# A twelve-stage decoder on one Trainium2 core: the quantised feed-forward stage with its weights quantised in the stage before, the gate's products first, and the gate's chain laid into up's products

## What is computed

```python
def act_qdq(x):
    scale = jnp.maximum(jnp.max(jnp.abs(x)) / 32767.0, 1e-12)
    return jnp.clip(jnp.round(x / scale), -32768.0, 32767.0) * scale
def fixed_qdq_u16(x):
    return jnp.clip(jnp.round(x * 65536.0), 0.0, 65535.0) / 65536.0
x = act_qdq(_layernorm(x))
up = act_qdq(x @ lpbq_dequant(w_up).T)       # weights in blocks of 32, 4 bits
gate = act_qdq(x @ lpbq_dequant(w_gate).T)   # 768 features each
sig = fixed_qdq_u16(jax.nn.sigmoid(gate))
gate = act_qdq(gate * sig)
o = act_qdq(gate * up)
return o @ lpbq_dequant(w_down).T            # added to x
```

## Time and profile before

| | |
|---|---|
| median of 3 runs | 2941.95 us (2939.73 to 2943.08) |
| profiled execution, its own time | 2943.42 us |
| its span | 2941.7 us |
| busy | PE 74%, DVE 60%, ACT 41%, POOL 19% |
| mean granted TensorE clock | 0.861 |

### The profile page before, as it was taken

The page is one execution under the profiler, slowest core; times in us unless marked ns, Lnnn a source line. Parts: engine busy times, 40 slices in busy tenths (PEclk is TensorE's granted clock), DMA queues, the critical chain, the costliest instruction groups (busy, mean ns, idle before and its releaser), DMA issues. The chain is left out here.

```text
span 2941.7 us, 28763 instructions
## 1 busy us (share of the span) xinstructions
PE 2190.0 (74%) x10262; PEld 1365.5 (46%) x10293; DVE 1775.1 (60%) x2543; ACT 1191.5 (41%) x1871; POOL 570.0 (19%) x332
## 2 busy tenths in 40 slices
PE   3788899694799889695648888887599483173794
PEld 2456556582233247574214444444357331162474
DVE  3455354425677555313669898987345656836765
ACT  1334322111466634111248898998132125301240
POOL 2231112121322110120105454642012000000100
PEclk8899799697899989697878999998699787586896
DMA  6644100253844000343000000001100000000001
GB/s 168 102 73 51 55 1 0 100 173 102 115 65 65 1 19 1 115 159 88 29 29 1 0 1 1 1 1 58 55 1 1 33 0 0 0 7 0 19 1 34
DMA packets 107530, 126.74 MB, mean 43 GB/s; under 512 B 14823, under 2 KB 98676, under 8 KB 106357
## 3 DMA queue, kind: packets, MB, share of 16 engines
q1 hardware_dynamic: 87444, 102.55, 15.8%
q10 hardware_dynamic: 17058, 14.79, 1.6%
q0 software_dynamic: 2880, 7.48, 0.7%
...
## 5 line engine op out<-in xcount | busy, mean ns | idle before, releaser
L2914 DVE TENSOR_TENSOR_SCAN l2s_h<-l2s_aw 128x2048 f32<-128x2048 f32 x64 | 283.5, 4430 | 3.3 <-PE l2s_c_ps L2863 2.7
L2871 PE MATMUL l2s_big<-g_xn,g_ident 128*128 128x512 f32 x512 | 266.8, 625 | 11.7 <-ACT g_xn L2947 5.8
L2928 POOL TENSOR_SCALAR l2s_aw<-l2s_aw 128x2048 f32<-128x2048 f32 x64 | 240.0, 3750 | 152.0 <-DVE l2s_aw L2906 147.1
L568 DVE TENSOR_REDUCE l1at_nm<-l1at_s 128x1 f32<-128x512 f32 x256 | 162.0, 684 | 63.9 <-PE l1at_s L418 62.9
L2863 PE MATMUL l2s_c_ps<-g_ident,l2s_h 128*128 128x128 f32 x1024 | 155.4, 287 | 45.7 <-ACT g_xn L2947 26.3
L2863 PEld LDWEIGHTS l2s_c_ps<-g_ident,l2s_h 128*128 128x128 f32 x1024 | 122.7, 147 | 141.3 <-issue 99.1
L2947 ACT ACTIVATE g_xn<-l2s_c_ps,l2sfr_ct 128x512 f32<-128x512 f32 x256 | 169.2, 736 | 35.0 <-PE l2s_c_ps L2863 33.9
L666 ACT ACTIVATE g_xn<-l1at_s 128x512 f32<-128x512 f32 x256 | 143.2, 598 | 81.8 <-PE l1at_s L442 81.3
L2906 DVE TENSOR_TENSOR l2s_aw<-l2s_dtu,l2s_b_ps 128x2048 f32<-128x2048 f32 x64 | 146.2, 2288 | 27.9 <-remote 22.1
L2940 ACT ACTIVATE l2s_aw<-l2s_dt,l2s_A 128x2048 f32<-128x2048 f32 x64 | 131.2, 2052 | 0.0
L568 DVE TENSOR_REDUCE l0at_nm<-l0at_s 128x2 f32<-128x384 f32 x128 | 70.1, 557 | 98.6 <-PE l0at_s L418 97.3
...
## 6 DMA issues: line engine op xcount, KB each, us to landing
...
```

Of the source, the lines that this page charges most:

```text
L568: V.tensor_reduce(nm[:, s % 2, qts[0]:qts[-1] + 1, r], s1[:, u % 3, 0:len(qts) * KEYS].rearrange("p (q k) -> p q k", k=KEYS), AX, ALU.max, ...
L2871: nc.tensor.matmul(acc[:, tb, :], ident[:], hCT[:, tb, :], start=n == 0, stop=n == NST - 1).then_inc(acc_done, 1)
L2914: V.tensor_tensor_scan(out=h_all[:, i % 2].rearrange("p c t -> p (c t)"), data0=dA[:, i % 2].rearrange("p c t -> p (c t)"), data1=wd[:, i ...
L2928: nc.gpsimd.tensor_scalar(wd[:, i % 3], wd[:, i % 3], 10.0, -10.0, ALU.min, ALU.max).then_inc(clipped, 1)
```

## The change

The weights get a scope of their own around both stages (`QuantisedBlocks`, tiles l2q). They are loaded by SP at the start of the cross-attention's tile loop, and VectorE quantises them in place in 15 pieces, one behind each tile's addition. `quantised_ffn` becomes one block, layer norm included. x's peak is taken over `xn`, two tiles at a time, between the tiles' scalings. Gate's products come before up's. Gate's chain (shift, back, sigmoid, round, clip, swish, peak) runs on VectorE, ScalarE and GpSimd while TensorE makes up's products; GpSimd does all of gate's backs, one shift, the clip (now one step, `cut`), and up's back. Up keeps no scale of its own: only the constant is subtracted, and the scales are folded into o's (`fold`). The subtraction of swish's constant goes into the product (`multiply`), the max with 0 and the product of sigmoid and gate into one operation (`swish`). The down product goes tile by tile: o is shifted and brought back 128 tokens at a time. `emptied` counts ScalarE's copies out of the ring of four banks.

```diff
+            if blocks is not None:
+                @block.sync
+                def _(sp):
+                    blocks.load(sp)
...
+                    if blocks is not None:
+                        blocks.quantise(dve, t)
...
+        if 0 < t <= 14:
+            dve.wait_ge(self.step, t)
+        if t < 3:
+            dve.wait_ge(self.loaded[t], 16)
+            v.tensor_reduce(self.peak[:, t], blocks(t), AX, ALU.max, apply_absolute_value=True).then_inc(self.step, 1)
+        elif t == 3:
+            v.tensor_scalar(self.peak[:], self.peak[:], 1.0 / 7.0, 1e-12, ALU.mult, ALU.max).then_inc(self.step, 1)
+        elif t == 4:
+            v.reciprocal(self.inv[:], self.peak[:]).then_inc(self.step, 1)
+        elif t < 8:
+            v.tensor_tensor(blocks(t - 5), blocks(t - 5), per_block(self.inv, t - 5), ALU.mult).then_inc(self.step, 1)
+        elif t < 10:
+            part = flat[:, (t - 8) * half:(t - 7) * half]
+            v.tensor_scalar(part, part, ROUND, ROUND, ALU.add, ALU.subtract).then_inc(self.step, 1)
+        elif t < 12:
+            part = flat[:, (t - 10) * half:(t - 9) * half]
+            v.tensor_scalar(part, part, -8.0, 7.0, ALU.max, ALU.min).then_inc(self.step, 1)
+        elif t < 15:
+            v.tensor_tensor(blocks(t - 12), blocks(t - 12), per_block(self.peak, t - 12), ALU.mult).then_inc(self.step, 1)
...
-            prepare(nc, name + "l", c, [
...
-                    ch.step(v.tensor_reduce(peak[:], blocks, AX, ALU.max, apply_absolute_value=True))
-                    ch.step(v.tensor_scalar(peak[:], peak[:], 1.0 / 7.0, 1e-12, ALU.mult, ALU.max))
-                    ch.step(v.reciprocal(inv[:], peak[:]))
-                    ch.step(v.tensor_tensor(qb, blocks, inv[:, :, None].to_broadcast([P, NB, QB]), ALU.mult))
-                    ch.step(v.tensor_scalar(q[:], q[:], ROUND, ROUND, ALU.add, ALU.subtract))
-                    ch.step(v.tensor_scalar(q[:], q[:], -8.0, 7.0, ALU.max, ALU.min))
-                    ch.step(v.tensor_tensor(qb, qb, peak[:, :, None].to_broadcast([P, NB, QB]), ALU.mult))
...
+        uses = [("w", n, j) for n in (1, 0) for j in range(FC // 2)] + [("xn", j) for j in range(PAIRS)]
+        uses += [("ff", 1, j) for j in range(NT)] + [("ff", 0, j) for j in range(NT)] + [("down", j) for j in range(FC // 2)]
+        number = {use: u for u, use in enumerate(uses)}
+        shifter = "dddaap"
...
+                def take(*use):
+                    u = number[use]
+                    if u >= 4:
+                        pe.wait_ge(emptied, u - 3)
+                    return ring[:, u % 4, :]
...
+                for n in (1, 0):
+                    for j in range(FC // 2):
+                        turn_w(n, j)
+                for g in range(PAIRS):
+                    turn_xn(g)
+                turn_peak(X)
+                spread(X)
+                for j in range(NT):
+                    if j < NBLK:
+                        pe.wait_ge(x_quantised, j + 1)
+                    product(1, j)
+                product(0, 0)
+                turn_peak(GATE)
+                product(0, 1)
+                spread(GATE)
+                for j in range(2, NT):
+                    product(0, j)
+                for j in range(FC // 2):
+                    turn_down(j)
+                for n in (UP, SWISH, OUT):
+                    turn_peak(n)
+                    spread(n)
+                pe.wait_ge(emptied, number["down", FC // 2 - 1] + 1)
                 for t in range(TILES):
-                    if t % QT == 0:
-                        pe.wait_ge(o_ready, t // QT + 1)
+                    pe.wait_ge(o_ready, t + 1)
...
+                def scaled_tiles(g):
+                    for i in (2 * g, 2 * g + 1):
+                        v.tensor_scalar(xn[:, i, :], x[:, i, :], mean[:, i:i + 1], rstd[:, i:i + 1], ALU.subtract, ALU.mult).then_inc(xn_ready, 1)
+                def peak_of(n, col, a):
+                    return v.tensor_reduce(peaks[:, n, col:col + 1], a, AX, ALU.max, apply_absolute_value=True)
+                def peak_of_tiles(g):
+                    dve.wait_ge(xn_ready, 2 * g + 2)
+                    return peak_of(X, g, flat_xn[:, 2 * g * DM:(2 * g + 2) * DM])
+                scaled_tiles(0)
+                for g in range(1, PAIRS):
+                    scaled_tiles(g)
+                    peak_of_tiles(g - 1)
+                ch.step(peak_of_tiles(PAIRS - 1))
...
+                shift_x(0)
+                for b in range(NBLK):
+                    if b + 1 < NBLK:
+                        shift_x(b + 1)
+                    back_x(b)
...
+                for m in range(FC):
+                    if shifter[m] == "d":
+                        v.tensor_scalar(gate[:, m, :], gate[:, m, :], scale[:, GATE, 1:2], ROUND, ALU.mult, ALU.add).then_inc(shifted["d"], 1)
...
+                def swish(m):
+                    dve.wait_ge(sig_cut, m + 1)
+                    v.scalar_tensor_tensor(out=gate[:, m, :], in0=sig[m % 3], scalar=0.0, in1=gate[:, m, :], op0=ALU.max, op1=ALU.mult).then_inc(swish_made, 1)
+                def swish_peak(m):
+                    dve.wait_ge(swish_made, m + 1)
+                    return peak_of(SWISH, m, gate[:, m, :])
+                for m in range(FC - 1):
+                    peaks_of_products(UP, up, 0, m)
+                    swish(m)
+                    swish_peak(m)
+                ch.step(peaks_of_products(UP, up, 0, FC - 1))
+                begin_scale(UP, NT)
+                swish(FC - 1)
+                row_of_scale(UP, 1e-12)
+                end_scale(UP)
+                ch.step(swish_peak(FC - 1))
+                begin_scale(SWISH, FC)
+                row_of_scale(SWISH, 65536e-12)
+                end_scale(SWISH)
+                v.tensor_scalar(gate[:, 0, :], gate[:, 0, :], scale[:, SWISH, 1:2], ROUND, ALU.mult, ALU.add).then_inc(swish_shifted_d, 1)
+                ch.step(v.tensor_scalar(fold[:, 0:1], row[0:1, SWISH, 0:1], row[0:1, UP, 0:1], 1.0 / 65536.0, ALU.mult, ALU.mult))
+                ch.step(v.tensor_scalar(fold[:, 1:2], fold[:, 0:1], 1.0 / QMAX, None, ALU.mult))
...
+                def multiply(m):
+                    if m == 0:
+                        dve.wait_ge(swish_shifted_d, 1)
+                    else:
+                        dve.wait_ge(swish_shifted, m)
+                    dve.wait_ge(up_back, m + 1)
+                    v.scalar_tensor_tensor(out=up[:, m, :], in0=gate[:, m, :], scalar=ROUND, in1=up[:, m, :], op0=ALU.subtract, op1=ALU.mult).then_inc(product_made, 1)
...
+                shift_o(0)
+                for t in range(TILES):
+                    if t + 1 < TILES:
+                        shift_o(t + 1)
+                    back_o(t)
+                    if t >= 2:
+                        add(t - 2)
...
+            @block.gpsimd
+            def _(pool):
+                def back(m):
+                    wait_shifted(pool, m)
+                    nc.gpsimd.tensor_scalar(gate[:, m, :], gate[:, m, :], ROUND, scale[:, GATE, 0:1], ALU.subtract, ALU.mult).then_inc(gate_back, 1)
+                def cut(m):
+                    pool.wait_ge(sig_rounded, m + 1)
+                    nc.gpsimd.tensor_scalar(sig[m % 3], sig[m % 3], ROUND + 65535.0, ROUND, ALU.min, ALU.subtract).then_inc(sig_cut, 1)
+                back(0)
+                back(1)
+                nc.gpsimd.tensor_scalar(gate[:, FC - 1, :], gate[:, FC - 1, :], scale[:, GATE, 1:2], ROUND, ALU.mult, ALU.add).then_inc(shifted["p"], 1)
+                for m in range(FC):
+                    if m + 2 < FC:
+                        back(m + 2)
+                    cut(m)
+                for m in range(FC):
+                    pool.wait_ge(up_shifted, m + 1)
+                    nc.gpsimd.tensor_scalar(up[:, m, :], up[:, m, :], ROUND, None, ALU.subtract).then_inc(up_back, 1)
...
+                done = 0
+                for j in range(NT):
+                    empty(up[:, j // NBLK, j % NBLK * BANK:(j % NBLK + 1) * BANK], "ff", 0, j)
+                    if j == 2:
+                        shift_gate(3)
+                    elif j == 3:
+                        shift_gate(4)
+                    while done < 2 * FC and 4 + done * 20 // (2 * FC) <= j:
+                        if done % 2 == 0:
+                            sigmoid(done // 2)
+                        else:
+                            round_sigmoid(done // 2)
+                        done += 1
...
+                shift_up(0)
+                shift_up(1)
+                for m in range(1, FC):
+                    shift_swish(m)
+                    if m + 1 < FC:
+                        shift_up(m + 1)
...
+        with Scope(nc, "l2q") as S8:
+            blocks = QuantisedBlocks(nc, S8, of("L2_ffn_")) if stage(8) else None
+            if stage(7):
+                l2x = of("L2_xattn_")
+                c["norm"] = ("l2b", (l2x["g_x"], l2x["b_x"]))
```

(3 more changed lines are left out.)

327 lines of the change are left out of this document (181 added, 146 removed).

## The result

| | before | after |
|---|---|---|
| median | 2942.51 us (4 runs, 2939.73 to 2943.92) | 2895.85 us (4 runs, 2891.41 to 2898.39) |
| ratio to before | | 0.9844, 95% interval 0.9831 to 0.9858 |
| profiled execution, its own time and span | 2943.42, 2941.7 us | 2897.5, 2895.8 us |
| mean granted TensorE clock | 0.861 | 0.869 |

What follows compares the result with a forecast made beforehand. Stage 8 was read as stretches bound alternately by VectorE and TensorE, so overlap was the gain: last addition from 2610.68 to 2521.9, 88.8 us less 0.5, gives 2855.1 profiled, 2854 us median (3.0% faster), range 2846 to 2872.

Steps and rivals of the forecast that it cites:

- Weights in the loop, cost nothing: Cross-attention loop: weight-quantising pieces hide in 3.7 us of slack, turn stays 7.76 us; only the last tile costs 0.5.
- Up to the first product: From cross-attention's last addition to gate's first product: terms sum to 23.8 us, first product at 2330.0, 34.8 us earlier.
- Gate's products, T: Gate's products take 43.0 us, to 2373.0; gate's scale follows 4.4 us later, at T = 2377.4.
- Down: Down product after o's scale: 1.95 us of pieces, 16 tiles in 41.4, slow start 2.5; last addition at 2521.9.
- the rival of the low clock: TensorE granted no more than 0.50 in both product phases and down: slower than before, 2972 if all is lost; 1%.
- one sign of being wrong: Listed signs against the forecast included TensorE waiting for ScalarE's copies of up and a granted clock under 0.9 in products.
- GpSimd's price: GpSimd operations on 128x2048 floats: 1.9 us of work each, from the scan's clip, excluding VectorE's two-input and double-rate operations.
- gate's scale to swish's: Gate's chain beside up's products, VectorE the bound after its first swish: 62.7 us, swish's scale at 2440.1.
- swish's scale to o's: VectorE's shift, fold, six products and peaks, and o's scale: 35.3 us where before took 40.15, ending at 2475.4.
- GpSimd slow by itself: GpSimd's operations take 3.8 us of their own: first cut ends at T+20.3, time 2858 to 2866; 8%.
- The change doesn't overlap: Up's products stall on ScalarE, whose chain waits for GpSimd; up's 41 us come on top, 2895; 2%.
- The lock falls badly every time: Each of six swishes and six multiplies waits a whole 1.9 us GpSimd operation, 22.8 us in all: 2872; 12%.

Runs made afterwards that it cites:

- short pairs: The changed kernel with all three kinds of GpSimd pieces rewritten as operation pairs measured short (add/multiply, min/max), cut's offset moved into VectorE's multiply: 2836.86 us, 0.9651 of before.

## Why the prediction was wrong

**What held.**
- *Weights in the loop, cost nothing*: turn 7.76 us, 23.2 us more when they are taken out.
- *Up to the first product*: forecast 2330.0, measured 2328.06. Of the 1.9 us, 0.9 is an earlier start of the scalings (2313.76 for 2314.68), with a hand-over between the stages of 0.35 us, and 1.0 that two scalings and a peak took 1.24 us where the sum has 1.36, eight times.
- *Gate's products, T*: forecast 2377.4, measured 2376.30 (2376.14 and its 0.16).
- *Down*: from o's scale to the last addition forecast 46.5 us, measured 46.4. The terms that the prediction writes out (1.95, 41.4, 2.5) make 45.9; the other 0.6 has no term of its own there, and the last addition takes 0.42.
- *Clock*: 0.95 in gate's products, 0.93 in down; the rival of the low clock didn't come. In up's products one sign of being wrong did show: behind TensorE's waits for a bank (3.7 to 6.0 us) the granted clock fell from 0.98 (2389.00 to 2405.70) to 0.70 (2434.17 to 2451.00), between its two levels of 2.4 and 1.2 GHz. With short pairs, where it works on, it was 1.00 up to 2415. Swish's scale did not wait for it.

**What failed** is the step "GpSimd's price": "So I take 1.9 us for work". It took the scan's clip as the price of any scalar operation on 128x2048 floats. The clip is min/max, one of the four short pairs found; only one of the change's 19 GpSimd operations (the shift) has a short pair. Of the twelve backs and cuts the first took 9.2 us, beginning beside VectorE's shifts, and the others 7.1 to 7.2; the six of up took 5.7 in the mean. Two terms carry the miss:

| stretch | forecast | change | short pairs |
|---|---|---|---|
| gate's scale to swish's | 62.7 | 103.3 | 58.2 |
| swish's scale to o's | 35.3 | 41.7 | 34.0 |

That is 40.6 and 6.4 us, 47.0. T was 1.1 us early, so the last addition came 45.8 us after its forecast of 2521.9 (2567.68). The profiled execution came only 42.4 us after its own forecast (2897.5 for 2855.1): 0.5 is the allowance for the last tile, and 2.9 lie behind the stage, where the same code took 328.1 us for 331.0. With short pairs both terms come out a little under the forecast, and TensorE makes up's products there in 38.0 us without a gap, so the rest of the two sums held as a whole: the order of work, ScalarE's and TensorE's room, VectorE as the bound behind the first swish.

The price reached the time in two ways. Up to the last cut it is GpSimd's own pace. From swish's scale to o's it is the lock: VectorE works 40.1 of the 41.7 us and no multiply waits for its piece of up, but the shift takes 4.17 us and five of the six multiplies 5.31 or 3.40 in place of 2.28, beside the long pieces of up.

The rival "GpSimd slow by itself" named the right mechanism, and had too small a price: it took 3.8 us, the median of the clip in the scan, as GpSimd's own time. Its sum for the first cut, "five operations and 1.3", gives T + 34.0 with what the five took (9.2, 7.2, 2.0, 7.2, 7.1, and 1.4). The row showed how long one form takes; nothing in the profile of before bounded the others from above. The rival "The change doesn't overlap" is half of what happened: TensorE did stall on ScalarE's copies behind GpSimd. But up's products were through at 2440.4, 39 us ahead of swish's scale, so they did lie beside the chain. That the measured time is beside this rival's 2895 is chance: its 41 us were to be up's products, and the 47 are GpSimd's.

**The lock** was the part that the prediction weighed against a page. In the change a swish is held by a back: it starts 0.03 us after the back's start and ends 6.71 us after it. The Trainium skill, page "SBUF — State Buffer", section "Who interferes with whom", has the loser block for the whole instruction and keeps reductions out of it. The runs agree on reductions, and on copies and scalar operations (6.9 of 7.1 us); they differ for two-input operations, which were let through at 4.4 of 7.1. By its rule a swish would by estimate have taken 7.1 + 2.3 less 0.03, 9.4 us, where 6.68 was measured.

How much a lock costs depends on the length of what holds it, so the short pairs removed most of it too: in the fastest version the longest swish is 3.43 us and the longest multiply 3.54. The rival "The lock falls badly every time" had the count nearly right for the change and the price wrong: four of six swishes (6.59 to 6.68 us) and five of six multiplies are held, for 1.1 to 4.4 us each and not for 1.9. The holds of the first three swishes are hidden, since VectorE waits 2.85 us for the next cut all the same; behind the fourth it waits for no cut any more, so that hold is part of the 40.6 us.

**What stays open.** Why just these pairs are short is not settled; nothing here looks inside GpSimd. The four were found at 128x2048 float32 alone, with constants and, for the back, a scale column. Nor was the folding of the offsets or of up's scale tried by itself; it is covered only by the sums that came out.
